# Two cross-attention and feed-forward layers: the subtraction products move behind the score products in each half-step, with a rearranged opening and a rearranged border between the layers

## What is computed

```python
x = x + _L0_xattn_ref(_layernorm(x), ctx, ctx, ...)   # 16 heads of 8, layer norms, softmax, gate, output norm
x = x + _L0_ffn_ref(_layernorm(x), ...)               # silu(x w1) * (x w2), gelu, gelu, w3; hidden size 512
x = x + _L1_xattn_ref(_layernorm(x), ctx, ctx, ...)   # 16 heads of 8, plain softmax attention
x = x + _L1_ffn_ref(_layernorm(x), ...)               # relu(x W1 + b1) W2 + b2
```

```python
scores = einsum('bqhd,bkhd->bhqk', q, k) * scale
attn = softmax(scores, axis=-1)
out = einsum('bhqk,bkhd->bqhd', attn, v)
```

## Time and profile before

| | |
|---|---|
| runs | 950.07, 953.3, 954.53 us; median 953.3 |
| the profiled execution | 954.53 us, of which 952.7 us from the first to the last instruction |
| TensorE busy | 918.2 us (96%) |
| ScalarE busy | 772.2 us (81%) |
| VectorE busy | 699.4 us (73%) |
| GpSimd busy | 325.6 us (34%) |
| 44 to 256 us, steady attention of layer 0 | TensorE 210.23, ScalarE 187.49, VectorE 182.02 us of 212 |
| 256 to 618 us, feed-forward of layer 0 | TensorE 356.92, ScalarE 303.05, VectorE 243.57 us of 362 |
| 635 to 840 us, attention of layer 1 | TensorE 196.17, ScalarE 149.25, VectorE 139.47 us of 205 |

### The profile page before, as it was taken

One profiled execution on the slowest core, in us unless ns is written; L12 is line 12 of the kernel. 1 busy time (PEld: TensorE's weight loads), 2 busy tenths in 40 slices (PEclk: granted clock), 3 DMA queues, 4 the chain that ended last, 5 costly groups with the idle time before them and its releaser, 6 DMA issues.

```text
span 952.7 us, 33022 instructions
## 1 busy us (share of the span) xinstructions
PE 918.2 (96%) x12342; PEld 712.8 (75%) x12349; DVE 699.4 (73%) x2046; ACT 772.2 (81%) x1409; POOL 325.6 (34%) x543
## 2 busy tenths in 40 slices
PE   6999999999989999999999999999999999999998
PEld 3687777787668888888788888767777777678886
DVE  7789998887776667666667666566766667589985
ACT  6798988889778988888888888667877777678985
POOL 5668888885530000000000000254444443021110
PEclk9999999999999999999999999999999999999999
DMA  6333322211000000000000000122222221100111
GB/s 210 94 102 96 103 76 84 75 49 45 5 1 1 1 0 0 0 0 0 0 0 0 0 0 1 56 82 74 73 63 65 67 68 54 25 2 34 44 45 56
DMA packets 54884, 41.72 MB, mean 44 GB/s; under 512 B 24416, under 2 KB 49248, under 8 KB 54752
## 3 DMA queue, kind: packets, MB, share of 16 engines
q1 hardware_dynamic: 53584, 37.12, 13.1%
q10 hardware_dynamic: 1168, 2.77, 0.8%
HBM read 16.79 MB, written 4.19 MB: 22 GB/s over the span
## 4 chain that ended last, share of the span: by engine, by line
PE 89%; DVE 4%; issue 3%; ACT 2%; DMA 1%; SPq 1%; ACTq 0%; POOL 0%; DVEq 0%; POOLq 0%
PE ps_w L1175 15%; PE ps_w L1174 15%; PE ps_w L579 7%; PE ps_av L634 6%; PE ps_w L576 5%; PE ps_w L562 4%; PE ps_mid L690 3%; PE ps_av L668 3%; PE ps_mid L549 3%; PE ps_y L677 3%; PE ps_mid L550 3%; PE ps_turn L644 2%; PE ps_turn L596 2%; PE g_ps_out L1174 2%; PE g_ps_out L1175 2%
## 5 line engine op out<-in xcount | busy, mean ns | idle before, releaser
L923 DVE TENSOR_REDUCE top<-ps_w 128x16 f32<-128x1024 f32 x128 | 155.9, 1218 | 94.6 <-PE ps_w L576 93.8
L1174 PE MATMUL ps_w<-g_h_lo,w_hi 128*128 128x512 f32 x512 | 206.7, 404 | 1.8 <-DVE g_h_lo L1429 1.7
L1175 PE MATMUL ps_w<-g_h_hi,w_hi 128*128 128x512 f32 x512 | 202.8, 396 | 0.0
L1429 DVE TENSOR_TENSOR g_h_lo<-g_h,g_h_hi 128x512 fp32r<-128x512 f32 x192 | 132.6, 690 | 87.2 <-ACT g_h_hi L1367 83.3
L133 POOL TENSOR_TENSOR front_rstd<-front_spread,minus_half 128x4 f32<-128x4 f32 x33 | 36.3, 1100 | 388.7 <-DVE front_spread L126 388.7
L733 ACT ACTIVATE prob_t<-ps_w 128x1024 f32<-128x1024 f32 x128 | 130.8, 1022 | 18.6 <-PE ps_w L579 18.0
L576 PE MATMUL ps_w<-qk_sets,qk_t 32*64 32x256 f32 x2048 | 143.9, 387 | 0.1
L1367 ACT ACTIVATE g_h_hi<-g_h 128x512 fp32r<-128x512 f32 x192 | 121.3, 632 | 18.6 <-DVE g_h L1439 14.4
L579 PE MATMUL ps_w<-qk_sets,qk_t 32*64 32x256 f32 x2048 | 134.2, 375 | 0.5 <-issue 0.5
L1174 PEld LDWEIGHTS ps_w<-g_h_lo,w_hi 128*128 128x128 f32 x512 | 96.7, 189 | 25.2 <-DVE g_h_lo L1429 3.5
L1175 PEld LDWEIGHTS ps_w<-g_h_hi,w_hi 128*128 128x128 f32 x512 | 96.9, 189 | 21.4
(11 more groups left out here) (165 smaller groups left out, 2011.2 us busy)
## 6 DMA issues: line engine op xcount, KB each, us to landing
qk_sets<-qk_t SPq DMA_DIRECT2D x254, 64.0 KB, 1.9
ctx_in<-in_ctx SPq DMA_DIRECT2D x32, 128.0 KB, 3.0
ctx_in<-in_ctx_t SPq DMA_DIRECT2D x32, 128.0 KB, 2.6
out_x<-x_res SPq DMA_DIRECT2D x15, 256.0 KB, 2.0
x_res<-in_x SPq DMA_DIRECT2D x14, 256.0 KB, 3.7
shift<-pieces SPq DMA_DIRECT2D x128, 16.0 KB, 2.3
w_raw<-in_ff_weights SPq DMA_DIRECT2D x8, 256.0 KB, 3.6
w_raw<-in_ff_weights ACTq DMA_DIRECT2D x1, 768.0 KB, 9.1
```

The source lines that it names most:

```text
L923: nc.vector.tensor_reduce(out=top[:, i % 2, half, :], in_=bank_pair(half).rearrange("p (a q) -> p a q", q=SEQ), op=ALU.max, axis=AX.X).the ...
L1174: nc.tensor.matmul(out, w_hi, x_lo, start=first and w_lo is None, stop=False)
L1175: return nc.tensor.matmul(out, w_hi, x_hi, start=False, stop=last)
L1429: nc.vector.tensor_tensor(h_lo[level][:, o, :], h[:, o % 2, :], h_hi[level][:, o, :].bitcast(F32), ALU.subtract).then_inc(lo_ready[level], 1)
```

## The change

In `half_step` the subtraction products stand behind the score and shift products. The first shift product of a bank now starts the accumulation, and the subtraction products end it. They alone wait for the DMA of the maxima.

In the opening, the value slots are cleared by GpSimd (three at its start, one at step -3) and no longer by VectorE and ScalarE; ScalarE clears two operand slots at step -1 and one each at the ends of steps -1 and 0, where it cleared four at step -1; unit 0 is normalised before unit 1 is measured; ScalarE issues its half of unit 0's scatter after it took unit 1's transposes; two of the five early weight splits move from step -2 to steps 0 and 1; and there are 13 products of zeros for 28.

At the border, the values of unit 0 and the transposes of unit 2 are made within the last chunk of the feed-forward (`first_values`, `turn_third`), and ScalarE loads the exponential's table and copies the values before it takes the last output. Two places of `FILL` lose 3 products.

```diff
-EARLY_SPLITS = {-3: range(0, 3), -2: range(3, 5)}
+EARLY_SPLITS = {-3: range(0, 3), 0: range(3, 4), 1: range(4, 5)}
-FILL = ({(-3, 0): 4, (-2, 0): 2, (-1, 0): 2, (-1, 1): 10, (0, 1): 4, (1, 0): 2, (1, 1): 4},
-        {(0, 0): 2, (1, 0): 2, (1, 1): 6})
+FIRST_FILL = 4
+FILL = ({(-2, 0): 2, (-1, 0): 2, (-1, 1): 3, (1, 0): 2},
+        {(1, 0): 2, (1, 1): 5})
...
 # open_scalar
-    clear_values(nc, t, op, slice(FIRST_SLOTS, UNROLL))
 # open_gpsimd
+    nc.gpsimd.memset(t.v_by_head[:, 0:UNROLL - 1, :, :], 0.0).then_inc(op.values_cleared, 1)
 # open_tensor, behind the bias products
+    keep_streaming(nc, t, stream, FIRST_FILL)
 # open_weights
-    nc.vector.memset(t.v_by_head[:, 0:FIRST_SLOTS, :, :], 0.0).then_inc(op.chain, 1)
...
 # half_step
                 if on(i):
-                    wait(pe, shift_landed[i % 2], landed(i, 2, PER_TILE))
                     wait(pe, top_ready, 2 * min(i + 2, N - 1) + turned_half + 1)
                     wait(pe, exp_done, 2 * (i - 1) + turned_half + 1)
-                    for b in range(PER_TILE):
-                        for g in (2 * turned_half, 2 * turned_half + 1):
-                            rows = slice(32 * g, 32 * (g + 1))
-                            nc.tensor.matmul(ps_w[b * SEQ:(b + 1) * SEQ, g * 512:(g + 1) * 512], t.halves[rows, b, :],
-                                             shift[rows, i % 2, :], start=True, stop=False)
...
-                                shifted = nc.tensor.matmul(out, qk_t[rows, i % QKT, 1, at], qk_sets[rows, q_slot(i), :, at],
-                                                           start=False, stop=k == UNIT_TILES - 1)
-                if on(i):
-                    shifted.then_inc(shifted_done, 1)
+                                nc.tensor.matmul(out, qk_t[rows, i % QKT, 1, at], qk_sets[rows, q_slot(i), :, at],
+                                                 start=k == 0, stop=False)
                 if on(unit):
                     score.then_inc(scores_done, 1)
+                if on(i):
+                    wait(pe, shift_landed[i % 2], landed(i, 2, PER_TILE))
+                    for b in range(PER_TILE):
+                        for g in (2 * turned_half, 2 * turned_half + 1):
+                            rows = slice(32 * g, 32 * (g + 1))
+                            shifted = nc.tensor.matmul(ps_w[b * SEQ:(b + 1) * SEQ, g * 512:(g + 1) * 512], t.halves[rows, b, :],
+                                                       shift[rows, i % 2, :], start=False, stop=True)
+                    shifted.then_inc(shifted_done, 1)
...
 # ScalarE, step(j)
-                if gated and j + 2 == 0:
-                    act.wait_ge(qk_taken, 1)
-                    scatter(act, 0, range(SETS // 2, SETS))
                 if j < 0 and j + 3 >= READY:
                     take_turned(j + 3)
+                if gated and j + 2 == 0:
+                    act.wait_ge(qk_taken, 1)
+                    scatter(act, 0, range(SETS // 2, SETS))
                 if gated and j == -1:
-                    clear_operands(nc, t, op, (slice(0, FIRST_OPERANDS.start), slice(FIRST_OPERANDS.stop, Q_SLOTS + K_SLOTS)))
+                    clear_operands(nc, t, op, (slot(q_slot(2)), slot(k_slot(2))))
...
+                if gated and j + 4 in (3, 4):
+                    clear_operands(nc, t, op, (slot(q_slot(j + 4)),))
...
 # VectorE, step(j)
+                if gated and j == -4:
+                    normalise(0)
...
 # GpSimd, step(j)
+                if gated and j == -3:
+                    nc.gpsimd.memset(t.v_by_head[:, UNROLL - 1:UNROLL, :, :], 0.0).then_inc(t.opening.values_cleared, 1)
...
 # gated feed-forward, last chunk: middle, down, ScalarE's step
+                    if level == 2 and last_chunk(i) and o == 2:
+                        first_values()
...
                 if final:
+                    turn_third()
                     pe.wait_ge(act_ready[LEVELS - 1], 4 * i + 4)
                     first_scores(1)
...
                 hidden(j, 2)
+                if last_chunk(j):
+                    open_exp()
+                    take_values(0)
```

More of the change, by code:

```diff
@@ L306, in clear_operands, with open_tensor @@
     last.then_inc(op.slots_cleared, 1)
[L309 to L318 removed]
+def open_tensor(nc, t, op, pe, stream):
     c = COLS
@@ L647, in step @@
                     project(j + 2)
-                if j < 0:
+                if j < 0 and j + 3 >= TURNED_IN:
                     turn_in(j + 3, j)
@@ L678, in step @@
                     last.then_inc(y_done, 1)
[L679 to L691 removed]
+                if on(j + 1) and j + 1 >= VALUED:
+                    values(j + 1)
                 if j >= 0:
@@ L782, in step @@
                     last.then_inc(ctx_normed, 1)
+                if j < 0 and j + 3 >= READY:
+                    take_turned(j + 3)
                 if gated and j + 2 == 0:
```

118 lines of the change are left out of this document (57 added, 61 removed).

## The result

| | before | changed |
|---|---|---|
| median of 20 runs each, us | 952.17 (949.33 to 957.68) | 960.50 (951.16 to 964.28) |
| mean of 20 runs, us | 952.33 | 958.77 |
| ratio, 95% interval | | 1.0069 (1.0052 to 1.0087) |
| profiled execution, us (span) | 954.53 (952.7) | 961.05 (959.3) |
| granted clock, whole span | 0.998 | 0.992 |

The changed kernel is 0.7% slower. The forecast was 953.7 us and no measurable change. On the 953.3 of the three runs shown the ratio makes 959.9, inside the range by 0.1 us (960.0); slower by over 0.5% had a chance of 0.18. That the range held is luck: its upper part stood for rivals 2 to 4, and what filled it was something else.

A forecast was written before the change was run, and what follows sets the result against it. TensorE was taken to bound the kernel, with 89% of the last-ending chain. Terms +6.8 - 1.7 - 0.6 - 3.2 - 0.9 = +0.4 on 954.5 us gave 954.9, forecast as 953.7 us at the median; 8-in-10 range 946.5 to 960.

The forecast's parts named there:

- Part A: Half-step order: +6.8 us on TensorE, -1.7 from waits for VectorE removed, -0.6 from subtractions' waits for a maximum.
- What the sum put at nothing: Half-step: exponentials on ScalarE get their input 0.055 us later, costed at nothing because probability-value products come half a step later.
- Part B: Opening: less clearing on VectorE and ScalarE and fewer fills bring -3.2 us, bounds -5.2 and 0.
- part C: Border between layers: table load and first values ahead of the feed-forward's last output bring -0.9 us, bounds -1.8 and +0.6.
- Its push of 0.5 on the last output: Border: table load and first values on ScalarE push the feed-forward's last output back by 0.5 us.
- 0.7 stay: Opening: of 1.7 us, including 0.9 us of fills, most is taken back by splits, clears and maxima; 0.7 us gain remains.
- one fill less, 0.2: Border: one filling product fewer on TensorE, booked as a gain of 0.2 us.
- Rival 3: Opening gains nothing: a later clock rise costs projections and scores before 26 us up to 3 us; 956.9 us, chance 0.10.
- Rival 1: Half-step: the new order costs TensorE nothing more, so the 6.8 us go; 946.9 us, chance 0.21.
- Rival 2: Half-step end: closing products' weight loads are not hidden, 0.10 us more per half-step; 966 us, chance 0.12.
- Rival 4: Half-step: the scores' earlier signal to VectorE does not come, 2.3 us go; 956.0 us, chance 0.57 together with the main case.

The follow-up runs named there:

- e3: The changed kernel with the old table of filling products behind its four new ones; 953.02 us, ratio to before 1.0021.
- e5: The changed kernel with the old order in the half-step and the old filling products; 947.92 us, ratio to before 0.9961.
- e6: The changed kernel with 15 one-column products added at TensorE's idle start; 954.30 us, ratio to before 1.0031.
- e8: The changed kernel with the old half-step order, its few fills and 15 one-column products at the start; 948.53 us, ratio to before 0.9970.
- e11: The changed kernel with old half-step order, old fills and 32 one-column products at the start; 950.73 us, ratio to before 0.9980.
- e1: The kernel before with only the new order inside the half-step; 955.35 us, ratio to before 1.0055.
- e7: The changed kernel with the old fills and the border between the layers undone; 954.26 us, ratio to before 1.0029.
- e2: The changed kernel with the old order in the half-step, opening, border and few fills kept; 950.69 us, ratio to before 1.0008.
- e12: The changed kernel with old half-step order, old fills and 64 one-column products at the start; 952.64 us, ratio to before 1.0003.
- e10: The kernel before with 113 one-column products added at TensorE's idle start; 957.01 us, ratio to before 1.0045.

## Why the prediction was right and wrong

1. *Part A, +6.8 - 1.7 - 0.6 = +4.5.* Right in size and mechanism. Floors 7.16 and 6.50 as forecast; first pass 0.27, subtraction 0.21 behind the last start, maximum at 1.23 for a forecast 1.2, five of the six waits gone. Measured +4.1 alone (mean +4.9), and 5.8 each as e3 less e5 and e6 less e8. What the sum put at nothing is a wait for the exponential: in the first steps of the second attention TensorE waits for it twice, 0.8 us in all, in each of the five profiles with the new order, and in those with the old one only once, 0.4 us in e11.
2. *Part B, -3.2, and part C, -0.9.* Together -4.1 forecast, -4.0 measured in e5. Projection of unit 2 at 23.15 for a forecast 23.7. The sum has this from VectorE, GpSimd and ScalarE alone. It has no term for a clock that rises sooner, at 12.8 us for 17.1 (10.3 to 13.8 in the profiles with the new opening, 14.2 to 17.1 with the old), so the closeness is in part luck. C gave 0.7. Its push of 0.5 on the last output came as forecast; with it the projection stands 1.05 us behind where the output would have been taken, for a forecast 1.3. The border and the second attention lose three filling products, not the one that part C counts.
3. *The step that failed: what 15 fills fewer do.* The sum books them as a gain: "0.7 stay" in part B and "one fill less, 0.2" in part C. In all they are a loss, 6.5 us by the medians and 4.7 by the means, between the change and e3. The booked gain itself is there: with the clock kept and the program's length restored, few fills are 1.2 us (e6 against e3) and 0.7 us (e8 against e5) better than many. What the sum left out is two costs:
   - The clock, about 4 us of the mean. Rival 3 named the clock and the fills, had them at 0.10, and priced them at 956.9, but with another course: "Should TensorE rise later, the projections and scores before 26 us cost up to 3 us more". TensorE rose sooner. What came is a second fall, at 23 us and lasting almost to 37, so that work far behind those products ran at the lower level too. By the groups of runs it comes in eleven of twenty, and the groups are 7.4 us apart.
   - The supply of instructions. "Its steps are uneven for reasons that the trace doesn't name; I leave these as they are" was the other mistake: an unnamed cost that depends on the program's length doesn't stay as it is when 15 products go. In the changed kernel's profile it is 4.7 us in the first attention, where e3 has 0.4; taking it out gains 1.8 us in the mean where the clock is kept, 3.0 in the kernel with the old order.
4. *Rival 1* is refuted by e1. *Rival 2* too: the subtraction starts 0.21 us after the last fp32 start in the same tiles, and a step is 7.16, not 7.35. The Trainium skill, "TensorE: Matmul & The Clock Gate", section on packing small matmuls, says in one place that a weight load overlaps only under another row group, and in another that one for the background weight buffer goes ahead too. This load shares row group and tiles and costs nothing more, so the measurement decides against the first; whether the second is what happens, no run here shows. *Rival 4* is refuted by the maximum at 1.23.

Put together by the means: +4.9 to 5.6 for the order (e1; e3 less e5), -3.8 for opening and border (e5), +4.7 for the fills (the change less e3), which makes 5.8 to 6.4, and the change is +6.4. Only the lower end, with e1, tests whether the parts add up; with e3 less e5 the sum is the change by construction. The 4.7 divide into 4.1 for the long fall (eleven of twenty runs, 7.4 us each), 1.8 for the pauses and 1.2 of gain. The old order divides alike: 2.3 for the fall (four of twelve runs, 7.0 each), 3.0 and 0.7. Each of these is good to about 2 us, and how often the fall comes is known from few runs (11 of 20, 5 of 12, 4 of 12, 3 of 12).

What starts a fetch late, and why the pause outlasts its landing by 1.15 to 1.67 us, no run here shows. Why two executions with the same idle times keep or lose the clock stays open too.

## What to carry to other kernels

Filling products look like cost at their place in the timeline; ask what clock they hold for the next ten microseconds before booking their removal as a gain, and look at all runs' clocks, not at one profile. Where the runs fall into groups, compare means and the groups, not medians. A change of a few instructions ahead of a long loop can move pauses of up to 1.7 us in and out of it, and from one loop to the next: add them up in every loop, and vary the program's length with one-column products in an idle stretch before you judge an edit worth under 1%.

## What the runs showed of the hardware

- Four 512-column fills took 1.87 us at 7.29 in the changed kernel, four at 33.42 took 1.03 in the kernel before. The windows print a clock of 1.00 for both, but the trace has no record of the clock ahead of 12.8 and 17.1 us; where the record begins, the products quicken (transposes 1.06 us at 15.07 before, 0.66 at 13.53 in the changed kernel). A 1.00 in the first windows is no reading.
- Products with tiny output cost little where TensorE is idle: 15 of one column 0.56 us, 113 of them 3.17, 28 ns each.
- TensorE stood still in the middle of a series of like products for up to 1.7 us, with nothing to wait for but its instructions, and went on 1.15 to 1.67 us after a 16 KB block had landed.
- One core alone, and the same program, ran at 0.987 to 0.992 or at 0.997 to 1.000 of full clock over the span, 7.4 us apart; in the one profile of the lower group this is one fall, from 23.0 to 36.7 us.
- Short falls of the clock (0.50 from 17.7 to 21.1 us in e3) came in the openings of seven of fourteen profiles. In four pairs of profiles with the same opening, one-column products apart (e3 and e7, e8 and e2, e11 and e5, e12 and e5), the one with the fall has its first probability-value product 1.6 to 1.7 us later; in e10 and the kernel before it is 0.2, where the clock of e10 had risen 3 us sooner.
